# Softmax attention on one core: value products of two key tiles in one visit, four buffers of exponentials

## The chip, the cores and the metric

One core of one Trainium2 chip. The metric is the device time of one execution of the program, in microseconds (us). Less than about 0.5% of it can't be told from no change.

## The reference

A two-layer block over `x` (16 batches, 56 rows, 128 features) with a context of 1500 rows a batch: linear attention, a quantized feed-forward, softmax attention, a mixture of 8 experts. The change lies in the softmax attention of the second layer. It has 16 heads of 8 features:

```python
scores = jnp.einsum('bhqd,bhkd->bhqk', qh, kh) / jnp.sqrt(jnp.float32(D_K))
scores = jnp.where(m == 0, jnp.float32(NEG_INF), scores)
attn = jax.nn.softmax(scores, axis=-1)
context = jnp.einsum('bhqk,bhkd->bhqd', attn, vh)
```

followed by an output projection with W_o. Here q comes from the normalized `x`, k and v from the context, and the mask is over the 1500 keys.

## The kernel before

The program is one unrolled stream of instructions for each engine, with semaphores between them. It has three stages: the linear attention over the context of all batches and the feed-forward (up to about 328 us), the softmax attention (328 to about 766 us), and the experts. All of the change is in the second.

**Windows and tiles.** The softmax attention runs 16 windows, one for each batch, written as pairs (`pair1`): the first and the last pair are unrolled, those between are a loop on each engine. A window has T = 12 key tiles of TK = 125 keys. The scores are held transposed, keys on partitions: for one tile `scores` (line 578) does 8 matmuls of 112 columns (two heads' 56 queries), four in each of two halves, into PSUM banks 0, 1 (even tiles) or 2, 3 (odd tiles). ScalarE turns both banks into exponentials in one instruction (`exponentials`, line 818, the activation on line 825) and writes them to one of two buffers `P[t % 2]`, 125 x 896 in float32. `weigh` (line 594) multiplies the values of the tile, `Vp`, with them: 8 matmuls (16 instructions in the profile, as they are float32) of 32 stationary columns each, placed in four column groups of the array, which add into PSUM bank 7 over the 12 tiles. `Vp` has a column of ones, so that the sums of the exponentials come out with the products. This text calls one call of `weigh` a value product.

**Units.** Between the scores and the value products TensorE does other work of the neighbouring windows, one unit at a time, in a list written out by hand (`PLACES`, lines 55 to 57). In window w:

- MX0 to MX20: plain score products (line 492) for window w+1, 128 queries x 500 keys each, of which VectorE takes the maximum (line 1222). From the maxima comes the shift of the exponentials.
- SH: the row of shifts (line 502), which VectorE copies into the stack of queries QS of window w+1 (line 1228).
- DEN and WO: the division by the sums and the output projection of window w-1 (lines 507 and 513); VectorE takes DEN with a reciprocal (line 1231) and WO with a copy.
- K0 to K2: the key projection for window w+2 (line 478). ScalarE takes it (line 776), VectorE makes the remainder (`key_rest`, line 1099).
- V0 to V2: the value projection for window w+1 (line 484), which ScalarE copies into `Vp` (line 769).

MX, SH, DEN and WO share PSUM banks 4 and 5 by turns: each waits until VectorE has emptied the unit two before it. K and V share bank 6, one at a time. Each tile has three places for units:

```python
PLACES = [["MX0", "MX1", "V0"], ["MX2", "MX3", "MX4"], ["DEN", None, "V1"], ["MX5", "MX6", "V2"],
          ["MX7", "WO", "K0"], ["MX8", "MX9", "MX10"], ["MX11", "MX12", "K1"], ["MX13", "MX14", "MX15"],
          ["MX16", "MX17", "K2"], ["MX18", "MX19", "MX20"], [None, None, None], ["SH", None, None]]
```

**Order on TensorE** (`window`, line 606): for each tile t, the first half of its scores, the unit of place 0, the second half, the unit of place 1, the value product of tile t-1 (in tile 0: of tile 11 of the window before), the unit of place 2. TensorE takes its instructions in this order, and an unmet wait holds all that stands behind it.

**Waits.** Scores of tile t wait for the exponentials of tile t-2 (their banks), exponentials of tile t for the scores of t and the value product of t-2 (their buffer), the value product of t for the exponentials of t. The first scores of a window also wait for the row of shifts and for the transfers of the stacks. After the exponentials of tile 0, ScalarE takes the finished sums of the window before (`take_sums`, line 829); the value product of tile 0 waits for that, as it writes the same bank.

**Transfers.** The scores use keys and queries stacked in bfloat16 parts. GpSimd makes the last part of the keys of window w+1 (line 918) after ScalarE's part (line 781), which it casts at tile 10 of window w-1. Then SP issues six transfers that stack the keys (line 335, 375 KB each), six that stack the queries (line 339), and the load of the context for window w+2 (line 327).

The tiles `xn` and `t0` (128 x 8 x 128, float32) are used by the normalizations before and after the softmax attention, not in it.

Of the kernel before, what the change touches and what calls it, by code (L numbers as in the profile page):

```python
# [6 lines left out]
ACT = mybir.ActivationFunctionType  # L7
# [5 lines left out]
B, S, D = 16, 56, 128  # L13
S2 = 1500
H, DK = 16, 8
T, TK = 12, 125
# [8 lines left out]
HQ = H * S  # L25
# [4 lines left out]
PAIRW = 2 * S  # L30
PW = 32
NPAIR = H // 2
SLOTS = 2 * NG
KVW = D + H
EPS_LN, EPS_IN = 1e-5, 1e-6
ROUND = 12582912.0
# [31 lines left out]
def units(w, of=None):  # L68

    if not isinstance(w, int):  # L70
        now = ALL
    elif w < 0:
        now = EARLY + MXS + ["SH"]
    elif w >= B - 1:
        now = ENDS
    else:
        now = [u for u in ALL if not (w == 0 and u in ENDS) and not (w == B - 2 and u[0] == "K")]
    return [u for u in now if of is None or kind(u) == of]
# [40 lines left out]
def in_pairs(eng, body, pairs):  # L119

    body(0)
    with eng.Fori(1, pairs - 1) as i:
        body(i)
    body(pairs - 1)


def build(nc, xh, ctxT, m0, m1, gates, rows, bq, bk, wkv0, wq0, dense0, wg0, wu0, wd0, wq1, wk1, wv1, wo1,
          gatew, w1, b1, w2, b2, bv, ident_in, hmask_in, hmask1_in, pmask_in,
          den_sel_in, rank_in, out):
    with ExitStack() as ctx:  # L130
        def sb(name, shape, dt=F32):
            return ctx.enter_context(nc.sbuf_tensor(name, shape, dt))
# [3 lines left out]
        def sem(name):  # L136
            if name not in sems:
                sems[name] = ctx.enter_context(nc.semaphore(name))
            return sems[name]
# [3 lines left out]
        xn = sb("xn", [128, NT, D])  # L143
        t0 = sb("t0", [128, NT, D])
# [46 lines left out]
        cT = [sb(f"cT{n}", [128, S2]) for n in range(2)]  # L191
        kvall = sb("kvall", [128, B, KVW])
        kvtmp = sb("kvtmp", [128, 2, D])
# [39 lines left out]

        Qb = [sb(f"Qb{n}", [128, H, S], BF16) for n in range(2)]
        Vp = [sb(f"Vp{n}", [128, T, NPAIR, PW]) for n in range(2)]
        P = [sb(f"P{n}", [128, HQ]) for n in range(2)]
        mx = sb("mx", [128, CH, KC])
        mneg = sb("mneg", [128, CH], BF16)
        O = sb("O", [128, 2 * PAIRW])
# [149 lines left out]
        def _(pe):  # L389
# [23 lines left out]
            def y_group(b, par, g, first):  # L413
                n = NG * b + g
                if g == 0:
                    pe.wait_ge(sem(f"ctx0_in{par}"), loads(b, par))
                if first:
                    if g == 0:
                        pe.wait_ge(sem("wkv_ready"), 1)
                    if g == 2:  # L420
                        pe.wait_ge(sem("q0T_ready"), 2)
                else:
                    pe.wait_ge(sem("kn_ready"), n - 2)
                    pe.wait_ge(sem("vn_ready"), n - 2)
                for t in range(GT):
                    c0 = (GT * g + t) * TK
                    ins = nc.tensor.matmul(ps2[0:TK, 1024 * g + 256 * t:1024 * g + 256 * t + 256],  # L427
                                           cT[par][:, c0:c0 + TK], wkv[:].rearrange("p k d -> p (k d)"),
                                           start=True, stop=True)
                ins.then_inc(sem("y_ready"), 1)  # L430
# [13 lines left out]

            pe.sem_inc(sem("kv_done"), SLOTS)
            y_group(0, 0, 0, True)
# [72 lines left out]
            for b in range(B):  # L519
                t, r = b // 2, HALF * (b % 2)  # L520
                ins = nc.tensor.matmul(ps[r:r + HALF, t // 3, KVW * (t % 3):KVW * (t % 3) + KVW],
                                       qT[:, HALF * b:HALF * b + HALF], kvall[:, b, :], start=True, stop=True)
# [55 lines left out]
            def scores(b, par, t, k, first):  # L578

                n = b * T + t  # L580
                if t == 0 and k == 0:
                    pe.wait_ge(sem(f"stacked{par}"), loads(b, par, 2 * STACK))
                    pe.wait_ge(sem(free_of(b - 1, "SH")), emptied(b - 1, "SH"))
                if k == 0 and not (first and t < 2):
                    pe.wait_ge(sem("p_ready"), n - 1)
                for p in range(4 * k, 4 * k + 4):
                    c0 = S2 * p + TK * t
                    ins = nc.tensor.matmul(ps[:, 2 * (t % 2) + k, PAIRW * (p % 4):PAIRW * (p % 4) + PAIRW],  # L588
                                           KS[par][:, c0:c0 + 128], QS[par][:, PAIRW * p:PAIRW * p + PAIRW],
                                           start=True, stop=True)  # L590
                if k == 1:
                    ins.then_inc(sem("sc_ready"), 1)

            def weigh(b, par, t, first):
                n = b * T + t
                pe.wait_ge(sem("p_ready"), n + 1)
                if t == 0 and not (first and par == 0):
                    pe.wait_ge(sem("o_ready"), b)
                for p in range(NPAIR):
                    r, c = PW * (p % 4), PAIRW * (p // 4)  # L600
                    ins = nc.tensor.matmul(ps[r:r + PW, 7, c:c + PAIRW], Vp[par][0:TK, t, p, :],  # L601
                                           P[t % 2][0:TK, PAIRW * p:PAIRW * p + PAIRW],
                                           start=(t == 0 and p < 4), stop=(t == T - 1), skip_group_check=True)
                ins.then_inc(sem("pv_done"), 1)

            def window(w, par, first_pair):

                def unit_at(t, place):
                    unit = PLACES[t][place]
                    if unit in units(w):  # L610
                        b = w - 1 if unit in ENDS else w + 2 if unit[0] == "K" else w + 1
                        fill(w, unit, b, par if unit[0] == "K" else 1 - par)

                first = first_pair and par == 0
                for t in range(T):
                    scores(w, par, t, 0, first)
                    unit_at(t, 0)
                    scores(w, par, t, 1, first)
                    unit_at(t, 1)
                    if t > 0:  # L620
                        weigh(w, par, t - 1, first_pair)
                    elif not first:
                        weigh(w - 1, 1 - par, T - 1, first_pair)
                    unit_at(t, 2)

            pe.wait_ge(sem("filled"), 1)
# [6 lines left out]
                    window(2 * i + par, par, fixed and i == 0)  # L633

            in_pairs(pe, pair1, B // 2)
            weigh(B - 1, 1, T - 1, False)
            fill(B, "DEN", B - 1, 1)
            fill(B, "WO", B - 1, 1)

# [67 lines left out]
        def _(act):  # L707
# [26 lines left out]
            def deviation(n, k):  # L734
                act.wait_ge(sem("ss_ready"), n + 1)
                nc.scalar.activation(sdk[0:TK, k % 2, :], ss[0:TK, k % 2, :], ACT.Sqrt,
                                     bias=eps_in[0:TK, :]).then_inc(sem("sdk_ready"), 1)
# [10 lines left out]
            def pair(i):  # L748
                first = isinstance(i, int) and i == 0
                for par in range(2):  # L750
                    for g in range(NG):
# [3 lines left out]
                        if not (first and k < 1):  # L755
                            values(n - 1, (k - 1) % SLOTS)
                        deviation(n, k)

            in_pairs(act, pair, B // 2)
            values(NG * B - 1, SLOTS - 1)  # L760
            act.wait_ge(sem("setup_in"), 80)
# [56 lines left out]
            def exponentials(b, par, t, first):  # L818
                n = b * T + t
                act.wait_ge(sem("sc_ready"), n + 1)  # L820
                if not (first and t < 2):
                    act.wait_ge(sem("pv_done"), n - 1)
                act.wait_ge(sem("kb_ready"), 1)
                src = ps[0:TK, 2 * (t % 2):2 * (t % 2) + 2, 0:HQ2]
                nc.scalar.activation(P[t % 2][0:TK, :].rearrange("p (k n) -> p k n", k=2), src, ACT.Exp,  # L825
                                     scale=kscale[0:TK, bass.ds(n, 1)],
                                     bias=kbias[0:TK, bass.ds(n, 1)]).then_inc(sem("p_ready"), 1)

# [127 lines left out]
        def _(dve):  # L956
# [89 lines left out]
            def state(b, par):  # L1046

                dve.wait_ge(sem("kv_done"), NG * (b + 1) + SLOTS)
                kv = ps[:, 6 + par, :]
                v.tensor_tensor(kvtmp[:, par, :], kv[:, 0:D], gmask[:], ALU.mult).then_inc(sem("kvt_ready"), 1)  # L1050
                v.tensor_scalar(kvall[:, bass.ds(b, 1), D:KVW], hmask[:].unsqueeze(1), kv[:, D + 1:D + 2], None,
                                ALU.mult)
# [4 lines left out]
            def pair(i):  # L1057
                first = isinstance(i, int) and i == 0
                for par in range(2):
                    b = 2 * i + par  # L1060
                    for g in range(NG):
                        n, k = NG * b + g, NG * par + g
                        norms(n, k)
                        if not (first and k < 2):
                            relu(n - 2, (k - 2) % SLOTS)
                        if g == 0 and not first:
# [4 lines left out]
            last = NG * B - 1  # L1071
            relu(last - 1, SLOTS - 2)
            relu(last, SLOTS - 1)
# [6 lines left out]
            def nd(t):  # L1080
                return ps[:, t // 3, KVW * (t % 3):KVW * (t % 3) + KVW]

            for t in range(NT):
                ins = v.tensor_scalar(xn[:, t, 0:H], nd(t)[:, D:KVW], EPS_IN, None, ALU.add)
            step(ins)
# [338 lines left out]
```

## Time and profile before

| what | us |
|---|---|
| runs | 888.0, 891.3, 892.58 (median 891.3) |
| profiled execution: span (no other time of this execution is given) | 888.3 |
| TensorE busy | 715.8 |
| VectorE busy | 590.6 |
| ScalarE busy | 482.0 |
| GpSimd busy | 251.1 |
| the softmax attention, first scores to the last window's end | 328 to 766 |

The profile names engines PE (TensorE's matmuls), PEld (its weight loads, which overlap the matmuls), DVE (VectorE), ACT (ScalarE), POOL (GpSimd) and SPq (SP's queue of transfers). A row of a timeline has the start, the length, the engine, the line, the operation with output <- input, the shapes and a count of merged instructions. In brackets stands how long the engine was idle before it and what ended that. The length of a merged row reaches from the first start to the last end; ends of matmuls are modelled and overlap the next start, so that the text goes by starts.

### The profile page before, as it was taken

What the parts mean: (1) busy time and instruction counts of PE and PEld (TensorE: products, weight loads), DVE (VectorE), ACT (ScalarE), POOL (GpSimd) and SP (SyncE); (2) the same over time, 40 slices, a digit from 0 to 9 for tenths busy, and PEclk for the clock granted to TensorE, in tenths of its full rate; (3) what the DMA queues carried; (4) which work ended last, traced back from release to release, by engine and by line L of the source; (5) the groups of instructions that cost most, each with busy time, mean ns of one, the idle gap of its engine ahead of it and who ended that gap; (6) DMA issues with size and microseconds to landing.
All of it is one profiled execution on the core that took longest, in us unless ns stands there. A gap on an engine that the chain in (4) does not pass through costs nothing.

```text
span 888.3 us, 19613 instructions
## 1 busy us (share of the span) xinstructions
PE 715.8 (81%) x7277; PEld 492.1 (55%) x7277; DVE 590.6 (66%) x1145; ACT 482.0 (54%) x718; POOL 251.1 (28%) x236
## 2 busy tenths in 40 slices
PE   1588888876436478986799999999999997699998
PEld 1466666665222225653565566666566664457776
DVE  7699999996678676754567676668677675421111
ACT  1366666663225316664567766767666675463332
POOL 7177777774100540220122102222202210000000
PEclk9899999997565759997999999999999999889999
DMA  3122222141770074894959898899998977011101
GB/s 121 35 70 70 69 69 69 69 147 35 58 87 1 0 118 74 103 126 68 106 92 126 116 127 118 122 125 123 122 139 101 126 80 113 10 48 47 47 26 33
DMA packets 59459, 74.16 MB, mean 83 GB/s; under 512 B 35308, under 2 KB 40166, under 8 KB 59422
## 3 DMA queue, kind: packets, MB, share of 16 engines
q1 hardware_dynamic: 59422, 73.65, 52.9%
q8 instruction: 25, 0.41, 0.2%
q14 instruction: 12, 0.10, 0.0%
HBM read 32.61 MB, written 1.40 MB: 38 GB/s over the span
## 4 chain that ended last, share of the span: by engine, by line
PE 48%; DVE 30%; issue 11%; DMA 5%; SPq 3%; ACT 3%; DVEq 1%; POOL 0%; ACTq 0%
PE ps L601 7%; PE ps L492 7%; DVE ss L1023 6%; PE ps L588 6%; PE ps L659 6%; PE ps L671 6%; DVE mx L1222 6%; PE ps L484 5%; PE ps L478 5%; DMA QS<-QD 3%; DVE arena L1038 3%; DVE arena L1044 2%; DVE xn L977 2%; PE ps L513 2%; DVE wv L1034 1%
## 5 line engine op out<-in xcount | busy, mean ns | idle before, releaser
L1222 DVE TENSOR_REDUCE mx<-ps 128x1 f32<-128x500 f32 x336 | 215.0, 674 | 115.4 <-PE ps L492 113.9
L825 ACT ACTIVATE P<-ps,kbias,kscale 125x896 f32<-125x896 f32 x192 | 210.4, 1097 | 97.3 <-PE ps L588 93.0
L918 POOL TENSOR_TENSOR KP<-kvall,KP 128x1500 bf16<-128x1500 f32 x16 | 48.5, 3031 | 344.8 <-ACT KP L781 344.8
L492 PE MATMUL ps<-KP,Qb 128*128 128x500 bf16 x336 | 135.3, 404 | 9.7 <-issue 4.4
L601 PE MATMUL ps<-P,Vp 125*32 125x112 f32 x3072 | 116.4, 269 | 3.1 <-issue 1.7
L427 PE MATMUL ps<-wkv,cT 128*125 128x256 f32 x384 | 91.9, 383 | 0.8 <-ACT arena L744 0.8
L601 PEld LDWEIGHTS ps<-P,Vp 125*32 125x32 f32 x3072 | 68.6, 110 | 42.9 <-issue 36.0
L441 PE MATMUL ps<-arena 125*128 125x130 f32 x384 | 57.6, 294 | 37.3 <-DVE arena L1044 34.5
L744 ACT ACTIVATE arena<-ps,wv 125x128 f32<-125x128 f32 x192 | 54.8, 368 | 58.0 <-DVE arena L1038 58.0
L441 PEld LDWEIGHTS ps<-arena 125*128 125x128 f32 x384 | 48.2, 196 | 56.1 <-DVE arena L1044 52.8
L588 PE MATMUL ps<-QS,arena 128*128 128x112 bf16 x768 | 67.5, 215 | 12.5 <-issue 6.1
L588 PE MATMUL ps<-QS,KS 128*128 128x112 bf16 x768 | 70.4, 218 | 9.0 <-DVE QS L1228 4.6
L588 PEld LDWEIGHTS ps<-QS,KS 128*128 128x128 bf16 x768 | 55.4, 101 | 39.8 <-issue 24.3
L902 POOL TENSOR_TENSOR arena<-arena,row 125x512 f32<-125x512 f32 x48 | 61.1, 1272 | 54.0 <-DVE arena L1038 54.0
L588 PEld LDWEIGHTS ps<-QS,arena 128*128 128x128 bf16 x768 | 52.7, 99 | 41.5 <-issue 25.6
L427 PEld LDWEIGHTS ps<-wkv,cT 128*125 128x125 f32 x384 | 69.2, 190 | 10.0 <-issue 1.2
L776 ACT ACTIVATE KP<-ps,bk_sb 128x500 bf16<-128x500 f32 x48 | 32.5, 677 | 76.3 <-PE ps L478 76.3
L869 ACT ACTIVATE arena<-ps,b 128x448 f32<-128x448 f32 x64 | 40.4, 633 | 47.9 <-PE ps L659 42.1
L478 PE MATMUL ps<-cT,wk_sb 128*128 128x500 f32 x96 | 58.4, 693 | 9.8 <-issue 6.7
L905 POOL TENSOR_TENSOR arena<-arena,row 125x512 f32<-125x512 f32 x48 | 64.2, 1337 | 3.8
L1338 DVE SCALAR_TENSOR_TENSOR t<-ps,pgd,t 128x128 f32<-128x128 f32 x56 | 16.0, 345 | 70.1 <-PE ps L671 70.1
L1023 DVE TENSOR_REDUCE ss<-arena 125x8 f32<-125x1024 f32 x48 | 57.9, 1205 | 3.6 <-ACT arena L731 3.6
(189 smaller groups left out, 1038.8 us busy)
## 6 DMA issues: line engine op xcount, KB each, us to landing
cT<-ctxT_dram SPq DMA_DIRECT2D x32, 750.0 KB, 4.4
KS<-KP SPq DMA_DIRECT2D x48, 375.0 KB, 12.9
arena<-KP SPq DMA_DIRECT2D x48, 375.0 KB, 12.9
QS<-QD SPq DMA_DIRECT2D x96, 28.0 KB, 15.9
wgu<-w_dram SPq DMA_DIRECT2D x8, 256.0 KB, 2.8
silu<-w_dram SPq DMA_DIRECT2D x8, 256.0 KB, 2.6
x<-xh_dram SPq DMA_DIRECT2D x1, 512.0 KB, 3.3
mixed<-att SPq DMA_DIRECT2D x16, 28.0 KB
```

What stands on the lines that cost most here:

```text
L427: ins = nc.tensor.matmul(ps2[0:TK, 1024 * g + 256 * t:1024 * g + 256 * t + 256], cT[par][:, c0:c0 + TK], wkv[:].rearrange("p k d -> p (k d)"),
L441: ins = nc.tensor.matmul(ps[:, 6 + par, 0:D + 2], KN[0:TK, s6, t, :], VN[0:TK, s6, t, :], start=(g == 0 and t == 0), stop=(g == NG - 1 and ...
L478: ins = nc.tensor.matmul(ps[:, bank, 0:KCW], wk1_sb[:], cT[par][:, KCW * k:KCW * k + KCW], start=True, stop=True)
L492: ins = nc.tensor.matmul(ps[:, bank, 0:KCW], q[:, 128 * c:128 * c + 128], KP[par][0][:, KCW * k:KCW * k + KCW], start=True, stop=True)
L588: ins = nc.tensor.matmul(ps[:, 2 * (t % 2) + k, PAIRW * (p % 4):PAIRW * (p % 4) + PAIRW], KS[par][:, c0:c0 + 128], QS[par][:, PAIRW * p:PA ...
L601: ins = nc.tensor.matmul(ps[r:r + PW, 7, c:c + PAIRW], Vp[par][0:TK, t, p, :], P[t % 2][0:TK, PAIRW * p:PAIRW * p + PAIRW], start=(t == 0 ...
L744: ins = nc.scalar.activation(VN[0:TK, k, t, 0:D], ps2[0:TK, c0:c0 + D], ACT.Copy, scale=wv[0:TK, k % 2, t:t + 1])
L825: nc.scalar.activation(P[t % 2][0:TK, :].rearrange("p (k n) -> p k n", k=2), src, ACT.Exp, scale=kscale[0:TK, bass.ds(n, 1)], bias=kbias[0 ...
L902: nc.gpsimd.tensor_tensor(kn, kn, bc(row[0:TK, GAMMA, :], 1, [TK, GT, D]), ALU.mult).then_inc(sem("kg_ready"), 1)
L905: nc.gpsimd.tensor_tensor(kn, kn, bc(row[0:TK, BETA, :], 1, [TK, GT, D]), ALU.add).then_inc(sem("kb0_ready"), 1)
L1023: v.tensor_reduce(ss[0:TK, k % 2, :], SQ[0:TK, k % 2, :].rearrange("p (j d) -> p j d", d=D), AX.X, ALU.add).then_inc(sem("ss_ready"), 1)
L1222: ins = v.tensor_reduce(mx[:, c, k:k + 1], ps[:, bank, 0:KCW], AX.X, ALU.max)
```

## The change

Every second tile does two value products, one after the other. In even tiles t that is those of t-2 and t-1 (in tile 0: of tiles 10 and 11 of the window before); odd tiles do none. After the last window the last two are done together. The exponentials get four buffers in place of two, `P[t % 4]`; the two new ones lie over `xn` and `t0`. The exponentials of tile t wait for the value product of t-4.

```diff
+PB = 4
...
-        P = [sb(f"P{n}", [128, HQ]) for n in range(2)]
+        P = [sb(f"P{n}", [128, HQ])[:] for n in range(2)]
+        P += [a[:].rearrange("p t d -> p (t d)")[:, 0:HQ] for a in (xn, t0)]
...
-                                           P[t % 2][0:TK, PAIRW * p:PAIRW * p + PAIRW],
+                                           P[t % PB][0:TK, PAIRW * p:PAIRW * p + PAIRW],
...
-                    if t > 0:
-                        weigh(w, par, t - 1, first_pair)
-                    elif not first:
-                        weigh(w - 1, 1 - par, T - 1, first_pair)
+                    if t % 2 == 0:
+                        for back in (2, 1):
+                            if t > 0:
+                                weigh(w, par, t - back, first_pair)
+                            elif not first:
+                                weigh(w - 1, 1 - par, T - back, first_pair)
                     unit_at(t, 2)
...
-            weigh(B - 1, 1, T - 1, False)
+            for back in (2, 1):
+                weigh(B - 1, 1, T - back, False)
...
-                if not (first and t < 2):
-                    act.wait_ge(sem("pv_done"), n - 1)
+                if not (first and t < PB):
+                    act.wait_ge(sem("pv_done"), n - PB + 1)
...
-                nc.scalar.activation(P[t % 2][0:TK, :].rearrange("p (k n) -> p k n", k=2), src, ACT.Exp,
+                nc.scalar.activation(P[t % PB][0:TK, :].rearrange("p (k n) -> p k n", k=2), src, ACT.Exp,
```

## Rows read from the trace of the kernel before

**Rows 1.** The page: TensorE's busy time, and the chain that ended last by engine.

```profile
PE 715.8 (81%) x7277; PEld 492.1 (55%) x7277; DVE 590.6 (66%) x1145; ACT 482.0 (54%) x718; POOL 251.1 (28%) x236
...
PE 48%; DVE 30%; issue 11%; DMA 5%; SPq 3%; ACT 3%; DVEq 1%; POOL 0%; ACTq 0%
```

**Rows 2.** By window: length; busy PE, PEld, DVE, ACT, POOL; clock; DMA share, GB/s.

```profile
453.84:480.64 26.80, 25.11 (x357) 16.36 (x358) 19.07 (x31) 19.07 (x21) 6.21 (x6) 1.00 0.91 116
...
586.77:613.03 26.26, 25.10 (x357) 16.36 (x358) 19.05 (x31) 18.00 (x21) 5.13 (x6) 1.00 0.94 125
613.03:639.84 26.81, 25.11 (x357) 16.37 (x358) 19.07 (x31) 19.08 (x21) 6.22 (x6) 1.00 0.92 120
...
692.88:720.68 27.80, 26.66 (x357) 17.50 (x358) 19.15 (x31) 18.11 (x21) 5.12 (x6) 0.94 0.81 94
```

**Rows 3.** Timeline, tiles 1 to 4 of the window at 586.77: start, length, engine.

```profile
589.49 0.37 PE L492 MATMUL ps<-KP,Qb 128*128 128x500 bf16 x1
...
591.22 0.65 PE L507 MATMUL ps<-O,den_sel 128*128 128x224 f32 x2
...
592.51 1.14 PE L484 MATMUL ps<-wv_sb,cT 128*125 128x128 f32 x8
...
593.69 0.62 ACT L769 COPY Vp<-ps 125x512 f32<-125x512 f32 x1 [0.39 <-PE ps L484]
...
594.92 1.14 PE L484 MATMUL ps<-wv_sb,cT 128*125 128x128 f32 x8
...
595.89 0.36 PE L588 MATMUL ps<-QS,arena 128*128 128x112 bf16 x4
...
596.09 0.37 PE L492 MATMUL ps<-KP,Qb 128*128 128x500 bf16 x1
...
596.30 0.36 PE L588 MATMUL ps<-QS,arena 128*128 128x112 bf16 x4
```

**Rows 4.** Timeline, tiles 5 to 7 of the same window.

```profile
599.26 0.37 PE L492 MATMUL ps<-KP,Qb 128*128 128x500 bf16 x1
...
601.65 0.10 PEld L492 LDWEIGHTS ps<-KP,Qb 128*128 128x128 bf16 x1 [0.24 <-DVE mx L1222]
...
601.97 0.35 PEld L601 LDWEIGHTS ps<-P,Vp 125*32 125x32 f32 x16 [0.22 <-issue]
...
602.49 0.30 PEld L478 LDWEIGHTS ps<-cT,wk_sb 128*128 128x128 f32 x2 [0.17 <-issue]
...
603.63 0.37 PE L492 MATMUL ps<-KP,Qb 128*128 128x500 bf16 x1
...
604.04 1.92 DVE L1222 TENSOR_REDUCE mx<-ps 128x1 f32<-128x500 f32 x3 [0.63 <-PE ps L492]
```

**Rows 5.** Timeline, tiles 9 to 11 of the same window and the next start.

```profile
608.00 0.37 PE L492 MATMUL ps<-KP,Qb 128*128 128x500 bf16 x1
...
611.21 0.37 PE L502 MATMUL ps<-identb,mneg 128*1 128x128 bf16 x8 [0.37 <-DVE mneg L1246]
...
611.63 1.27 DVE L1228 CAST QS<-ps 1x448 bf16<-1x448 f32 x2 [0.57 <-PE ps L502]
...
613.03 0.27 PE L588 MATMUL ps<-QS,KS 128*128 128x112 bf16 x2 [0.63 <-DVE QS L1228]
```

**Rows 6.** Timeline of TensorE cut inside one value product, and the whole product.

```profile
573.18 0.40 PE L601 MATMUL ps<-P,Vp 125*32 125x112 f32 x8
...
573.18 0.59 PE L601 MATMUL ps<-P,Vp 125*32 125x112 f32 x16
```

**Rows 7.** Line 339, 590 to 613.5: six query stacks, issue and time to landing.

```profile
L339 SPq DMA_DIRECT2D QS<-QD x6: 598/604/612, 594.4 to 597.6; - x6
...
DMA to landing us min/median/max: 15.2/16.2/17.3
```

**Rows 8.** Timeline of ScalarE in the last window.

```profile
759.34 2.12 ACT L825 ACTIVATE P<-ps,kbias,kscale 125x896 f32<-125x896 f32 x2 [0.16 <-PE ps L588]
```

**Rows 9.** Timeline of TensorE, a long gap in window 2.

```profile
407.68 2.04 PE L478 MATMUL ps<-cT,wk_sb 128*128 128x500 f32 x2 [6.70 <-issue]
```

## The prediction, made before the changed kernel ran

> **What bounds the kernel now.** I read the page first. [rows 1] TensorE is busy 81% of the span and the chain that ended last is 48% TensorE, 30% VectorE and 11% "issue": two engines hand work to each other, and no busy share alone says what an edit is worth. All of the change lies in the second attention, so the next view was the busy time by window (one batch of 12 key tiles, 16 in all, counted from 0) [rows 2]. Nine of them, from 453.84 to 692.88, take 239.04 us, 26.56 each, alternately 26.26 and 26.80, at full granted clock. The 16th has no maxima to make for a successor and is shorter.
>
> Then the timeline inside one window of 26.26 us. Five things are to be seen there.
>
> *Tiles 0 to 4* [rows 3]: TensorE goes from one operation to the next. The exception is tile 1: its three score products for the maxima (MX2, MX3, MX4) feed two PSUM banks that VectorE empties in 0.64 us each (three in 1.92, [rows 4]), and DEN at 591.22, which takes MX3's bank, starts 1.73 us after MX2 at 589.49, just when VectorE has got through MX2 and MX3 (0.41 until it starts, 2 × 0.64, 0.04 or so for the signal).
>
> *Tiles 5 to 8* [rows 4]: from MX8 at 599.26 to MX12 at 601.65 are 2.39 us, and MX12 waited for VectorE: 0.41 + three reductions in 1.92 + 0.06. From MX12 it is TensorE's turn: 0.32 to the value product, 0.52 for it, 1.14 for the key projection and four score products, and MX13 starts at 603.63, 1.98 us after MX12. VectorE idles 0.63 meanwhile. The pair of tiles 7 and 8 repeats it, in 4.37 us each.
>
> *Tiles 9 to 11* [rows 5]: from MX18 at 608.00 to the next window at 613.03 are 5.03 us, all of it behind VectorE: three reductions, the rest of the key parts, the largest of the maxima, and then, after TensorE's turn at 611.21, the row of shifts (two copies, 1.27 us, from 611.63), for which the next window's first scores wait. Three value products lie in that time and cost nothing.
>
> *One value product* [rows 6]: 16 instructions in 0.59 us, the first 8 in 0.40. So each 8 take 0.19 at the steady pace, though a product set between other operations displaces 0.52 behind it and 0.1 ahead of it: weight loads stand idle 0.22 before its own and 0.17 before the next operation's [rows 4].
>
> *The transfers* [rows 7]: the stacks of the queries for the window at 613.03 were issued from 594.4 to 597.6 and landed 15.2 to 17.3 us later, so by about 612.8. That is just in time. The issue starts after GpSimd's key remainder, which hangs on the end of the window before. This makes a second loop over two windows, of 26.26 + 26.80 = 53.06 us [rows 2], against 52.5 for the compute loop; it is what makes every other window 0.54 longer.
>
> **The change part by part.** No product is removed: a window has 6 double visits instead of 12 single ones. Odd tiles lose theirs; even tiles do that of t-2 and of t-1 (tile 0: tiles 10 and 11 of the window before).
>
> *A double visit* costs 16 more matmuls in an even tile. Bounds: 0.35 (the 16 weight loads of a block) and 0.52 (a whole lone block), both [rows 4]. I take 2 × 0.19 = 0.38, the steady pace, because nothing but already met waits stands between the two tiles.
>
> *Tile 0*: +0.38, on TensorE's path.
>
> *Tile 1*: the product goes, but MX4 needs MX2's bank and DEN needs MX3's: MX2 to DEN stays 1.73. 0.00. TensorE stands still where it worked.
>
> *Tile 2*: +0.38. DEN, scores and V1 are all TensorE's.
>
> *Tile 3* is the one real gain. V1 to V2 is 2.40 now (592.51 to 594.92). Without the product TensorE needs 0.98 for V1, four scores 0.20, MX5 0.21, four scores 0.20, MX6 0.21: 1.80 (0.98, 0.20 and 0.21 by 594.92, 595.89, 596.09 and 596.30). But V2 takes the one side bank that ScalarE empties: its copy starts 1.18 after V1 (593.69) and takes 0.62, with the signal 1.85. So the gain is 2.40 - 1.85 = 0.55.
>
> *Tile 4*: +0.38. The values' last part of ScalarE stays ahead of the next user.
>
> *Tiles 5 and 7*: the product lies between MX9 and MX10 (MX14 and MX15), inside the 2.39 us that VectorE sets: 0.00 for each. *Tiles 6 and 8*: the double visit lies after MX12 (MX17), where VectorE waits for TensorE: +0.38 each.
>
> *Tiles 9, 10, 11*: under VectorE's 5.03 us. The cover: tile 10's double visit would end near 610.8, the shifts come at 611.21. 0.00; without that cover it would cost another 0.4.
>
> Sum: 5 × 0.38 - 0.55 = **+1.35 us a window**: 27.61 for the compute loop.
>
> *The transfer loop*: only the stretch up to the window's end grows, by 1.35, so two windows need 53.06 + 1.35 = 54.41 by transfers and 55.22 by compute. It stops binding, and its 0.54 in every other window is swallowed.
>
> *Four buffers*: two are laid over tiles that are idle in this stage; no instruction is added. The exponentials wait for the product four tiles back instead of two. ScalarE isn't late: in tiles 5 to 8 it idles too, and tile t's scores wait for exponentials t-2 as before. The doubled visit ends each pair's use of exponentials later, which two more buffers cover; without them ScalarE would wait in each odd tile.
>
> *ScalarE and the queues*: ScalarE takes the finished sums after tile 0's visit, which ends 0.38 later; what it does next, the copy of V0, is 0.38 later by TensorE anyway. No DMA is moved and SP and GpSimd are passed by nothing.
>
> *Last window*: here ScalarE sets the pace: two exponentials in 2.12, then 0.16 idle, 2.28 a pair [rows 8]. With the change one exponential of each pair still comes after a product and eight scores: 0.00, at most 0.1 a pair.
>
> Total: nine windows 9 × 27.61 - 239.04 = +9.5. Windows 1 to 3, 13 and 14, whose starts show no transfer wait: 5 × 1.35 = +6.8. Window 0 has no visit in tile 0 and no DEN: +0.9. Sum **+17.2**. The profile has gaps "issue" of several us in some windows (one of 6.70, [rows 9]) which the change doesn't address. The profiled execution's span is 888.3; no other time of that execution is shown, and the span lies within the runs' 888.0 to 892.6, so I put the sum on the median: 891.3 + 17.2 = **908.5**.
>
> **A rule against the forecast.** The trace shows 0.22 and 0.17 us of idle weight loading around a product [rows 4]. The Trainium skill, TensorEngine Tiling (Array Packing), Key Properties, says that a change of tiling mode, though not of tile, drains the engine; these products use 32 of 128 columns and their neighbours 128. By that rule alone, with every saved drain on the path, the sum would be rival A's; the trace agrees that a switch costs something, 0.24 a pair by the terms above, but not that it is waited for.
>
> **The rivals.** *A, the saved switches reach the end (faster).* Place: each odd tile. Price: a visit costs 0.1 + 0.52, its second half in a double one 0.38, so 0.24 is saved six times a window, 1.4. That would need VectorE and ScalarE to be early enough at MX4, MX10, MX12, MX15, MX17 and V2; it decides if the 2.39 us shrink. By TensorE alone: 14 × 1.4 = 20 less. But of the 1.4, 1.2 lies ahead of the key part that releases the transfers, and that loop then needs (53.06 - 1.2)/2 = 25.9 a window, 0.6 less, in nine of them; with 5 × 1.4 in the others about 12 in all, **879**. For it: the idle loads. Against it: MX12's wait for VectorE in all windows. Chance 0.10. The Trainium skill's rule above, taken alone, gives the same.
>
> *B, the two cancel (no change).* Place: tiles 5 to 8. If the second half of the double visit is hidden there, under a VectorE that is late at MX13 too, the two +0.38 go and tile 3's gain stays: 3 × 0.38 - 0.55 = 0.6 a window, half of which the transfer wait swallows in nine of them: +6, **897**; with a gain of tile 1's half us it is 892. Against it: VectorE idles 0.63 ahead of MX13 [rows 4], more than the 0.38. Chance 0.13, 0.08 of it within 0.5%.
>
> *C, the clock falls as well.* TensorE works 1.4 us less and waits 2.8 more in each longer window. Window 13 had a granted clock of 0.94 and took 27.80 where its like takes 26.26 [rows 2]: 1.5 each. In six or more windows it makes **918** and up. Chance 0.07.
>
> *D, the second product isn't at the steady pace* (0.52, as alone): 75 visits × 0.14 = +10: **919**. Part of the forecast's upper end.
>
> **How the numbers follow.** Forecast 0.70, A 0.10, B 0.13, C 0.07. A measurement of this kernel can tell about 0.5% (4.5 us) from nothing. Slower by more: 0.70 + 0.07 + 0.05 of B = 0.82; within: 0.08; faster: 0.10. The lower bound of the visit (0.35) gives 906, gaps of "issue" move by some us in either direction; the range 896 to 917 takes in the upper half of B and part of C and D.
>
> **What would show it.** Right: windows of 27.6 without alternation; MX8 to MX12 still 2.39; MX12 to MX13 2.36 in place of 1.98; value products as 32 in about 0.97; V1 to V2 1.85; "DVE mx" as releaser of TensorE in tiles 1, 5, 7 for about 0.5 more; busy TensorE down by some 10 us at most. Wrong: MX8 to MX12 shorter, or windows under 26.3 (A); windows of 26.5 to 27 (B); granted clock under 0.95 in many windows (C); 32 matmuls in over 1.05 (D).

## The result and the profile after

| | before | after |
|---|---|---|
| runs, us | 888.0 to 892.58, median 891.44 (4) | 899.27 to 901.86, median 900.48 (4) |
| profiled execution: its time, its span | as in the table of before, 888.3 | 901.86, 900.1 |

The ratio is 1.011, with a 95% interval of 1.008 to 1.0139: the change makes the kernel slower by 9 us. The forecast was 908.5, in a range of 896 to 917. Between the two profiled executions the difference is 11.8 us of span; the profiled one of after was the slowest of its four.

TensorE does the same products in 5 us less busy time, and the span is 11.8 longer (the row of the page that answers to the first of [rows 1]):

```profile
PE 710.8 (79%) x7276; PEld 499.7 (56%) x7277; DVE 586.2 (65%) x1145; ACT 482.1 (54%) x718; POOL 251.2 (28%) x236
```

By window (the columns of [rows 2]):

```profile
457.24:484.70 27.46, 24.83 (x358) 16.82 (x358) 18.85 (x31) 18.54 (x21) 5.68 (x6) 1.00 0.90 118
...
594.42:621.82 27.40, 24.77 (x357) 16.82 (x358) 18.84 (x31) 18.55 (x21) 5.69 (x6) 1.00 0.90 118
621.82:649.22 27.40, 24.77 (x358) 16.83 (x358) 18.86 (x31) 18.55 (x21) 5.69 (x6) 1.00 0.90 118
...
731.42:762.30 30.88, 23.79 (x352) 16.47 (x352) 17.09 (x28) 15.89 (x17) 2.68 (x1) 0.89 0.85 116
```

The two things forecast of the windows are there. They are longer, 27.4 where the windows of before took 26.26 and 26.80 by turns, and the alternation is gone. The nine windows from the one that starts at 457.24 take 246.82 us (to 704.06) against 239.04: +7.8. Window 14, the last row, took 30.88 at a clock of 0.89, with a gap "issue" of 4.86 in it; its counterpart took 27.91 at 0.94, with a gap of 3.69.

The timeline of tiles 1 to 4 of the window at 594.42, which answers to [rows 3]:

```profile
597.52 0.37 PE L494 MATMUL ps<-KP,Qb 128*128 128x500 bf16 x1
...
598.67 0.38 PE L494 MATMUL ps<-KP,Qb 128*128 128x500 bf16 x1 [0.37 <-DVE mx L1227]
...
599.25 0.30 PEld L509 LDWEIGHTS ps<-O,den_sel 128*128 128x128 f32 x2 [0.16 <-DVE mx L1227]
599.25 0.65 PE L509 MATMUL ps<-O,den_sel 128*128 128x224 f32 x2
...
600.02 0.97 PE L603 MATMUL ps<-P,Vp 125*32 125x112 f32 x32
...
600.93 1.14 PE L486 MATMUL ps<-wv_sb,cT 128*125 128x128 f32 x8
...
602.78 0.95 PEld L486 LDWEIGHTS ps<-wv_sb,cT 128*125 128x125 f32 x8 [0.22 <-ACT Vp L774]
```

In tile 1 TensorE now stands still for VectorE 0.37 us ahead of MX4, and ahead of DEN its weight load waits for VectorE again (0.16); MX2 to DEN is 1.73 as before. The double visit is one block of 0.97, which holds up V1 by 0.91 (600.02 to 600.93). V1 to V2 is 1.85, with 0.22 of it a wait for ScalarE's copy of V1.

Tiles 5 to 7, which answer to [rows 4]:

```profile
607.50 0.37 PE L494 MATMUL ps<-KP,Qb 128*128 128x500 bf16 x1
...
607.92 1.85 DVE L1227 TENSOR_REDUCE mx<-ps 128x1 f32<-128x500 f32 x3 [1.88 <-PE ps L494]
...
608.65 0.39 PE L494 MATMUL ps<-KP,Qb 128*128 128x500 bf16 x1 [0.37 <-DVE mx L1227]
...
609.82 0.10 PEld L494 LDWEIGHTS ps<-KP,Qb 128*128 128x128 bf16 x1 [0.16 <-DVE mx L1227]
...
610.14 0.73 PEld L603 LDWEIGHTS ps<-P,Vp 125*32 125x32 f32 x32 [0.22 <-issue]
...
611.04 1.10 PE L480 MATMUL ps<-cT,wk_sb 128*128 128x500 f32 x2
...
612.18 0.37 PE L494 MATMUL ps<-KP,Qb 128*128 128x500 bf16 x1
```

MX12 to MX13 went from 1.98 to 2.36 us: the second product's 0.38. MX8 to MX12, which I had taken as fixed at 2.39, is 2.32. Three reductions take 1.85 in place of 1.92.

Tiles 9 to 11 and the next start, which answer to [rows 5]:

```profile
616.86 0.37 PE L494 MATMUL ps<-KP,Qb 128*128 128x500 bf16 x1
...
618.71 0.97 PE L603 MATMUL ps<-P,Vp 125*32 125x112 f32 x32
...
620.42 1.27 DVE L1233 CAST QS<-ps 1x448 bf16<-1x448 f32 x2 [0.57 <-PE ps L504]
...
621.82 0.37 PE L590 MATMUL ps<-QS,KS 128*128 128x112 bf16 x4 [1.15 <-DVE QS L1233]
```

MX18 to the next start is 4.96 (5.03 before). The double visit of tile 10, at 618.71, lies in its cover. The stacks of queries for the window at 621.82 landed by 605.8 + 15.2 = 621.0, 0.8 before it started ([rows 7]):

```profile
L341 SPq DMA_DIRECT2D QS<-QD x6: 598/599/604, 602.5 to 605.8; - x6
...
DMA to landing us min/median/max: 15.2/16.2/17.2
```

### The profile page after: what moved, and what is told of

Same layout as the page of the kernel before. It is cut to its first block, busy times and chain, and to the rows that moved or that the text cites. A ratio compares the mean times of both kernels' runs of the same rounds, so it can differ in the third digit from the quotient of the medians.

```text
span 900.1 us, 19642 instructions
## 1 busy us (share of the span) xinstructions
PE 710.8 (79%) x7276; PEld 499.7 (56%) x7277; DVE 586.2 (65%) x1145; ACT 482.1 (54%) x718; POOL 251.2 (28%) x236
## 4 chain that ended last, share of the span: by engine, by line
issue 43%; DVE 24%; PE 20%; POOL 5%; DMA 3%; SPq 2%; ACT 1%; DVEq 1%; POOLq 0%; ACTq 0%
DVE ss L1028 6%; PE ps L676 6%; PE ps L664 6%; DVE arena L1043 3%; POOL Qb L931 2%; DVE arena L1049 2%; DVE xn L982 2%; DMA QS<-QD 2%; POOL QD L935 1%; PE ps L494 1%; DVE wv L1039 1%; PE ps L603 1%; PE ps L395 1%; SPq L317 1%; DVE mx L1227 1%
## 5 line engine op out<-in xcount | busy, mean ns | idle before, releaser
L1227 DVE TENSOR_REDUCE mx<-ps 128x1 f32<-128x500 f32 x336 | 210.2, 672 | 131.7 <-PE ps L494 130.3
L494 PE MATMUL ps<-KP,Qb 128*128 128x500 bf16 x336 | 134.8, 403 | 28.5 <-DVE mx L1227 23.9
L830 ACT ACTIVATE P<-ps,kbias,kscale 125x896 f32<-125x896 f32 x96 | 105.4, 1097 | 55.8 <-PE ps L590 54.0
L443 PE MATMUL ps<-arena 125*128 125x130 f32 x384 | 58.5, 297 | 36.2 <-DVE arena L1049 33.4
L494 PEld LDWEIGHTS ps<-KP,Qb 128*128 128x128 bf16 x336 | 33.2, 99 | 69.2 <-DVE mx L1227 62.2
L830 ACT ACTIVATE xn<-ps,kbias,kscale 125x896 f32<-125x896 f32 x48 | 52.7, 1098 | 26.7 <-PE ps L590 26.7
```

What stands on the lines that cost most here:

```text
L443: ins = nc.tensor.matmul(ps[:, 6 + par, 0:D + 2], KN[0:TK, s6, t, :], VN[0:TK, s6, t, :], start=(g == 0 and t == 0), stop=(g == NG - 1 and ...
L494: ins = nc.tensor.matmul(ps[:, bank, 0:KCW], q[:, 128 * c:128 * c + 128], KP[par][0][:, KCW * k:KCW * k + KCW], start=True, stop=True)
L830: nc.scalar.activation(P[t % PB][0:TK, :].rearrange("p (k n) -> p k n", k=2), src, ACT.Exp, scale=kscale[0:TK, bass.ds(n, 1)], bias=kbias[ ...
L1227: ins = v.tensor_reduce(mx[:, c, k:k + 1], ps[:, bank, 0:KCW], AX.X, ALU.max)
```

## Experiments

The theory: a value product costs what its place makes it cost; in even tiles the double visit stands where TensorE is waited for, in odd tiles the room it leaves is filled by waits. Each run was made beside runs of the kernel before on the same chip, and ratios are to those. The times of whole executions move by several us with gaps "issue" and with the granted clock, so what is said of the mechanism rests on the lengths of single windows at full clock, which agree to 0.1 us inside an execution (transfer waits apart). "The nine steady windows" are windows 4 to 12, 239.04 us in the profile of the kernel before; what a kernel gains outside them can come from the gaps and the clock alone.

**Four buffers alone.** The value product is back in each tile:

```diff
-                    if t % 2 == 0:
-                        for back in (2, 1):
-                            if t > 0:
-                                weigh(w, par, t - back, first_pair)
...
+                    if t > 0:
+                        weigh(w, par, t - 1, first_pair)
```

> One value product in each tile as in the kernel before, but four buffers of exponentials, two of them over xn and t0, and exponentials that wait for the product four tiles back. Theory (place): the loss comes from where the double visits stand, the buffers cost nothing: windows of 26.26 and 26.80 by turns, 891 us, within 0.5% of the kernel before. Rival (buffers or ScalarE's waits): a part of the +9 us is here already, windows over 26.8 without alternation, 895 or more.

Measured: 888.86 us, ratio 0.9966 (0.9933 to 0.9999). The buffers cost nothing. Windows alternate as in the kernel before; some, like the third row, took 1.55 more at a clock of 0.94:

```profile
502.61:529.39 26.78, 25.10 (x358) 16.37 (x358) 19.06 (x31) 19.04 (x21) 6.18 (x6) 1.00 0.93 121
529.39:555.64 26.25, 25.09 (x357) 16.35 (x358) 19.05 (x31) 18.03 (x21) 5.15 (x6) 1.00 0.94 125
582.43:610.24 27.81, 26.65 (x357) 17.50 (x358) 19.14 (x31) 18.13 (x21) 5.14 (x6) 0.94 0.90 121
```

**Double visits one tile later.**

```diff
-                    if t % 2 == 0:
-                        for back in (2, 1):
-                            if t > 0:
-                                weigh(w, par, t - back, first_pair)
...
+                    if t == 0 and not first:
+                        for back in (2, 1):
+                            weigh(w - 1, 1 - par, T - back, first_pair)
+                    elif t % 2 == 1 and t > 1:
+                        for back in (3, 2):
+                            weigh(w, par, t - back, first_pair)
```

> The changed kernel with five of the six double visits one tile later: products of t-3 and t-2 in the odd tiles 3 to 11, that of the last two tiles in tile 0 as before. Same number of visits, same instructions. Theory (place): they now lie where TensorE waits for VectorE. Per window against the kernel before: tile 0 +0.38, tile 2 -0.62, tile 3 +0.38, tile 4 -0.62, tiles 5 and 6 -0.26, tiles 7 and 8 -0.26, MX20 late by 0.37, sum -0.6: compute loop 25.65, transfer loop (53.06 - 0.6)/2 = 26.2, so windows of 26.2 and about 885 us. Rival (a double visit costs its own time wherever it is put): windows of 27.4 and 900 us again.

Measured: 889.05 us, ratio 0.9967 (0.9939 to 0.9996). With as many double visits as the changed kernel, its execution has none of the loss; a double visit doesn't cost the same wherever it is put. But the windows are 26.7, not 26.2, so that 0.45 of the changed kernel's 1.14 over the compute loop of 26.26 is still there, and the nine steady windows take 240.8, no less than before:

```profile
586.61:613.32 26.71, 24.24 (x357) 16.58 (x358) 19.03 (x31) 18.26 (x21) 5.61 (x6) 1.00 0.93 123
613.32:640.10 26.78, 24.24 (x357) 16.59 (x358) 19.05 (x31) 18.39 (x21) 5.75 (x6) 1.00 0.92 120
```

The size was off for a wait that I had overlooked. In its timeline (tiles 7 and 8) the key projection at 606.76 waited for VectorE's remainder of the keys (line 1104), which empties bank 6 and comes only after three reductions, which the double visit had delayed. MX13 to MX18 (603.34 to 607.90) is 4.56, where I had worked out 4.11:

```profile
604.05 0.97 PE L603 MATMUL ps<-P,Vp 125*32 125x112 f32 x32
...
604.96 0.39 PE L494 MATMUL ps<-KP,Qb 128*128 128x500 bf16 x1
...
606.76 1.10 PE L480 MATMUL ps<-cT,wk_sb 128*128 128x500 f32 x2 [0.26 <-DVE kvall L1104]
...
607.90 0.37 PE L494 MATMUL ps<-KP,Qb 128*128 128x500 bf16 x1
```

**Products left out, in odd or in even tiles.**

```diff
                 pe.wait_ge(sem("p_ready"), n + 1)
+                if t in (2, 4, 6, 8, 10):
+                    pe.wait_ge(sem("pv_done"), n)
+                    pe.sem_inc(sem("pv_done"), 1)
+                    return
```

and the same with `(1, 3, 5, 7, 9)`.

> The kernel before without the products of key tiles 2, 4, 6, 8 and 10, which it does in tiles 3, 5, 7, 9 and 11; nothing stands in their place but the signal. Theory (place): they cost 0.55 in tile 3, 0.07 each in tiles 5, 7 and 9 and nothing in tile 11, 0.77 a window; nine windows go by transfers at (53.06 - 0.77)/2 = 26.15: about 883 us. Rival (TensorE is the bound, each product costs its 0.62): 3.1 a window, transfers at 25.2, about 865 us.

> The kernel before without the products of key tiles 1, 3, 5, 7 and 9, which it does in tiles 2, 4, 6, 8 and 10. Theory (place): 0.62 each in tiles 2, 4, 6 and 8, nothing in tile 10: 2.5 a window, transfers at (53.06 - 2.5)/2 = 25.3 in nine windows: about 869 us, nearly three times the gain of leaving out the same number in odd tiles. Rival (each product costs alike): the same time as without those in odd tiles.

Measured: 874.15 us (ratio 0.9796, 0.974 to 0.9853) without those in odd tiles, 870.29 (0.9759, 0.9705 to 0.9813) without those in even tiles. The totals don't decide between the theories: the first saved twice what I expected and the second about what I expected. The windows tell why. Without the products of odd tiles, and then window 2 of the kernel before:

```profile
379.69:408.10 28.41, 25.65 (x278) 16.33 (x278) 19.00 (x31) 17.67 (x20) 3.31 (x5) 0.89 0.88 117
...
517.09:543.85 26.76, 22.83 (x278) 14.61 (x278) 18.83 (x31) 19.07 (x21) 6.96 (x6) 0.98 0.91 118
543.85:571.98 28.13, 25.49 (x278) 16.36 (x278) 18.98 (x31) 18.12 (x20) 4.38 (x6) 0.89 0.89 119
```

```profile
384.47:420.69 36.22, 28.44 (x358) 18.05 (x358) 19.27 (x31) 18.17 (x21) 2.43 (x5) 0.83 0.69 92
```

Window 2 took 28.4 where the kernel before took 36.2. The gaps "issue" of over 1.2 us, five in the profile of the kernel before with 19.3 us together, are not in this one; why they went wasn't found out. The steady windows, meanwhile, are longer than before, up to 28.13: every second one waits over 2.4 us for transfers at its end, and in the next the granted clock is 0.89 to 0.94. The nine take 245.9 us without the products of odd tiles and 241.4 without those of even tiles, against 239.04: in neither kernel does any of the saving lie in them. What the products themselves cost is read inside a window. Without that of tile 3, V1 to V2 is 1.85 (-0.55, as expected). Without that of tile 5, tiles 5 and 6 take 4.29 in place of 4.37 (-0.08, as expected). In the kernel without the products of even tiles, tile 2 takes 1.89 in place of 2.54 (0.09 of which comes back in tile 3), tile 4 2.65 in place of 3.17, and tile 6 2.52 in place of 2.71: -0.19 and not the -0.62 expected. There the key projection waits for the remainder again:

```profile
564.13 1.10 PE L478 MATMUL ps<-cT,wk_sb 128*128 128x500 f32 x2 [0.26 <-DVE kvall L1103]
```

So in tiles 6 and 8 adding a product costs 0.38 but taking one away gives back 0.19: another wait stands right behind TensorE's work. What a product costs does hang on its tile: 0.56, 0.08 and 0.08 for those done in tiles 3, 5 and 7, and 0.57, 0.52, 0.19 and 0.19 for those in tiles 2, 4, 6 and 8.

**Earlier key stacks.** To read the compute loop by itself, the transfers were moved out of its way, in the kernel before and in the changed one:

```diff
-                sp.wait_ge(sem("kp3_ready"), b + 1)
                 for j, part in enumerate(KEY_PART):
+                    if j in (0, 5):
+                        sp.wait_ge(sem("kp2_ready" if j == 0 else "kp3_ready"), b + 1)
                     sp.dma_start(
```

> The kernel before, with the first five of the six transfers that stack the keys issued when ScalarE's part of them is there, and only the sixth waiting for GpSimd's remainder: the stacking starts about 2.8 us earlier in each window. Theory (the alternation of 26.26 and 26.80 is a wait for transfers, and 26.26 is the compute loop): all windows of 26.26, the stacks landed 2 us or more before a window starts, 2.4 us less in nine windows, about 0.3%. Rival (the alternation has another cause, or the transfers are bound by what they move and not by when they start): windows alternate as before and the time is the same.

> The changed kernel with the same earlier issue of the key stacks. Theory: its windows of 27.4 are set by TensorE and VectorE, the transfers have slack already, so nothing changes: windows of 27.40, within 0.3% of the changed kernel's 900.5. Rival (part of the loss is a wait for transfers): windows under 27.4.

Measured: 886.48 us, ratio 0.9926 (0.9903 to 0.9948), for the kernel before with it; 899.3, ratio 1.0081 to the kernel before (1.005 to 1.0112), for the changed one, whose own time was 900.48. Windows of the first, and its query stacks, landed by 611.3, 2.8 ahead of the start at 614.11:

```profile
561.58:587.85 26.27, 25.11 (x358) 16.38 (x358) 19.06 (x31) 18.54 (x21) 5.68 (x6) 1.00 0.94 124
587.85:614.11 26.26, 25.09 (x358) 16.36 (x358) 19.05 (x31) 18.53 (x21) 5.67 (x6) 1.00 0.94 124
```

```profile
L340 SPq DMA_DIRECT2D QS<-QD x6: 598/606/617, 592.9 to 596.1; - x6
...
DMA to landing us min/median/max: 15.2/16.2/17.3
```

A window of the second:

```profile
621.33:648.77 27.44, 24.81 (x357) 16.82 (x358) 18.84 (x31) 18.52 (x21) 5.67 (x6) 1.00 0.90 118
```

The compute loops are 26.26 and 27.44. The 0.54 in every other window of the kernel before was a wait for transfers, and the change hides it behind its own +1.18; the changed kernel gains nothing from earlier stacks. The nine steady windows of the kernel before gained 2.7 by them, where 2.4 was expected; its time fell by 0.7% where 0.3% was expected, and the rest of that isn't explained.

**Halves of the change.** With earlier stacks, double visits in tiles 0, 2 and 4 only; in tiles 6, 8 and 10 only; and in tile 4 only. A table says which tiles each visit takes:

```diff
+VISITS = [(2, 1), (), (2, 1), (), (2, 1), (1,), (1,), (1,), (1,), (1,), (1,), ()]
...
+                    for back in VISITS[t]:
+                        if t > 0:
+                            weigh(w, par, t - back, first_pair)
+                        elif not first:
+                            weigh(w - 1, 1 - par, T - back, first_pair)
```

> Kernel before with earlier key stacks (its windows then are 26.26), and the change in tiles 11 and 0 to 4 only: double visits in tiles 0, 2 and 4 (and for the last two tiles after the last window), single ones in tiles 5 to 10. Theory: tile 0 +0.38, tiles 1 and 2 +0.38, tile 3 -0.55, tile 4 +0.38: windows of 26.85. Rival (the double visits of tiles 6 and 8 carry the loss, the head breaks even): 26.3.

> Kernel before with earlier key stacks, and the change in tiles 5 to 10 only: double visits in tiles 6, 8 and 10, none in 5, 7 and 9, single ones elsewhere. Theory: +0.31 for each of the pairs 5, 6 and 7, 8 (0.385 for the second product, 0.075 back since MX10 and MX15 come in time), -0.075 for MX20: windows of 26.80, and with the other half the whole 1.14. Rival (the loss is all in the head): 26.3.

> Kernel before with earlier key stacks, and a single double visit: none in tile 3, the products of tiles 2 and 3 in tile 4. Theory (a double visit gains where TensorE is the one waited for at both places): +0.385 - 0.556 = -0.17 a window: 26.09. Rival (a double visit always loses): 26.3 or more.

Measured: the first 905.17 us, ratio 1.0153 (1.0043 to 1.0263), from two runs. Its second row is one of four windows of 28.3 to 28.5 at a clock of 0.94:

```profile
571.13:597.99 26.86, 24.81 (x357) 16.53 (x358) 19.08 (x31) 18.54 (x21) 5.67 (x6) 1.00 0.92 121
597.99:626.41 28.42, 26.37 (x357) 17.54 (x358) 19.16 (x31) 18.65 (x21) 5.66 (x6) 0.94 0.87 114
```

The second 889.97, ratio 0.998 (0.9946 to 1.0013), and the third 889.47, ratio 0.995 (0.9929 to 0.9971):

```profile
587.16:613.97 26.81, 25.05 (x357) 16.66 (x358) 18.83 (x31) 18.54 (x21) 5.67 (x6) 1.00 0.92 121
```

```profile
609.80:635.89 26.09, 24.93 (x357) 16.40 (x358) 19.06 (x31) 18.53 (x21) 5.67 (x6) 1.00 0.95 124
```

At full clock the windows are 26.86, 26.81 and 26.09: +0.60, +0.55 and -0.17 on 26.26, where 26.85, 26.80 and 26.09 had been worked out. The two halves add up to 1.15, all of the change's 1.14 to 1.18. One double visit in tile 4, with tile 3 left empty, shortens the window: there both products had been on TensorE's path, so that the saved switch counts. This holds of the windows and not of the totals. The half in tiles 0 to 4 came out no faster than the whole change (1.0153, on two runs, against 1.0081), with its windows at 0.94 and a gap "issue" of 6.26 in window 14, and the kernel with one double visit is no faster than the one with earlier stacks alone (0.995 against 0.9926), with a gap of 6.44 there.

**Products where TensorE waits.** The same table with other entries, without and with earlier stacks:

```diff
+VISITS = [(1,), (1,), (), (2,), (), (3,), (3,), (3,), (3,), (3,), (3, 2), (2, 1)]
```

> The kernel before with four buffers and the value products put where TensorE waits anyway: tiles 0, 1, 3, 5, 6, 7, 8 and 9 do one, tiles 2 and 4 none, tiles 10 and 11 two each. Same products. Theory (place): tile 2 gives about 0.57, tile 4 0.52, the rest stays, so the compute loop is 25.2; the transfer loop (53.06 - 1.1)/2 = 26.0 holds it back: about 881 us, with TensorE idle for over 2 us at window ends, after which the granted clock may fall for some us, as it did when products were left out: 881 to 888. Rival (the number of visits counts, not their place; here 12 products in 10 visits): at most 2 × 0.24 a window, about 886 with no dependence on place.

> The placement of the value products by waits, with the key stacks issued earlier as well. Theory: now neither the products nor the transfers hold the window back: windows of 25.2 to 25.4, 15 × 1.1 + 2.4 = 19 us less than before, about 872 us, granted clock 1.00 in the steady windows. Rival (the transfers are bound by what they move, 24.7 us of busy time a window): windows of 26 or more, 880 us or more.

Measured: 875.52 us, ratio 0.9805 (0.9768 to 0.9842), without earlier stacks, and **862.74, ratio 0.9671 (0.9642 to 0.97)**, with them. This version beats both kernels. Three windows without earlier stacks, then one with them:

```profile
577.09:602.27 25.18, 24.77 (x357) 16.43 (x358) 19.04 (x31) 17.77 (x20) 4.12 (x6) 1.00 0.98 130
602.27:629.06 26.79, 24.78 (x358) 16.43 (x358) 19.06 (x31) 18.85 (x21) 7.28 (x6) 1.00 0.92 120
629.06:655.74 26.68, 26.27 (x357) 17.64 (x358) 19.08 (x31) 17.76 (x20) 4.05 (x6) 0.94 0.94 126
```

```profile
567.55:592.72 25.17, 24.77 (x357) 16.43 (x358) 19.05 (x31) 18.30 (x21) 5.66 (x6) 1.00 0.98 129
```

The compute loop is 25.18, 1.08 less than 26.26 (1.1 expected). Without earlier stacks most windows wait for transfers up to 26.8, or run part of the time at the lower clock (third row): the nine steady ones take 239.09, as long as before, so that all of this version's gain (17 us, where 3 to 10 were expected) lies outside them. With earlier stacks the nine take 226.6, 12.4 less: 9 × 1.08 from the placement and 2.7 from the stacks. That the whole time fell by 30 us where 19 were expected comes from elsewhere: between the profiles windows 1 to 3 are 11.2 shorter where 3.3 was expected, with gaps "issue" of 9.7 in them in place of 14.4, and window 13 is 2.7 shorter where 1.1 was expected, as its counterpart ran at 0.94. With earlier stacks the DMA share is 0.98, so not much more is to be had that way.

## Why the prediction was right, and where its sizes were off

The direction, the mechanism and most terms held. Per window, at full clock:

| step of the prediction | forecast | measured |
|---|---|---|
| second product of a double visit | 0.38 | 0.38 (block of 0.97, MX12 to MX13 +0.38) |
| tile 0 | +0.38 | +0.38 |
| tiles 1 and 2 | 0.00 and +0.38 | -0.09 and +0.47, together +0.38 |
| tile 3 | -0.55 | -0.56 |
| tile 4 | +0.38 | +0.38 |
| tiles 5 and 6, 7 and 8 | +0.38 each pair | +0.31 each pair |
| tiles 9 to 11 | 0.00 | -0.08 |
| sum | +1.35 | +1.13 (windows: 27.40 - 26.26 = +1.14) |

(Measured in the windows at 586.77 and at 594.42: lengths of tiles, each from its first score product to that of the next.)

**The step that was mis-sized** is "Tiles 5 and 7 ... inside the 2.39 us that VectorE sets: 0.00". I read three reductions in 1.92 as VectorE at its own pace. It was not quite, and the 0.64 that I took for each is that mean: one takes 0.68, and two without a wait 1.25, so that one follows the other after 0.58 or so, as these rows of the kernel before show:

```profile
596.50 0.68 DVE L1222 TENSOR_REDUCE mx<-ps 128x1 f32<-128x500 f32 x1 [1.02 <-PE ps L492]
...
602.16 1.25 DVE L1222 TENSOR_REDUCE mx<-ps 128x1 f32<-128x500 f32 x2
```

The third waited some 0.07 for MX10, which the product had held back. Without the product the three take 1.85 (the timeline of tiles 5 to 7 above). The sign named for it, "MX8 to MX12 still 2.39", failed by as much, and the waits for "DVE mx" in tiles 1, 5 and 7 are 0.37 each instead of about 0.5. The product in an odd tile did cost 0.07, in three places a window: 0.22 of the 1.35, and some 3 us of the sum. What wait ends last had been read rightly for MX12, but the row of three merged reductions hid a wait inside it.

**The transfer loop** held: bound before, slack after, 0.54 swallowed in every other window (+7.8 in nine windows, where +9.5 was forecast; the difference is the term above, which alone would make 2.0).

**The other windows.** Windows 1 to 3, 13 and 14 took 6.2 more between the profiles (forecast 6.8), but partly by accident: windows 1 to 3 took 3.7 more, 3.0 is window 14 with its longer gap "issue" and lower clock, and window 13 took 0.4 less, since its counterpart had run at a clock of 0.94. Window 0, forecast +0.9, took 0.6 less: the kernel before had a gap "issue" of 1.24 in it. What follows the last window's start took 1.9 less, forecast 0; 0.7 of that is the last window up to its DEN. With 0.3 more ahead of window 0 these make 11.8 between the profiles; the medians differ by 9.0. Times move by that much from one execution to another: the 23 runs of the kernel before beside the first four experiments spread from 885.9 to 897.0, the shortest at a mean granted clock of 0.918, the longest at 0.906. Whether the gaps move too from run to run isn't on record, as each kernel has one profile.

**Rival A** (saved switches reach the end) had the prices of a single visit and of a second product right where TensorE is the one waited for: DEN to V1 is 0.61 shorter without the product done in tile 2, and a second product adds 0.38, which leaves about its 0.24. The one pair that was tried with both products on the path saved 0.17, as in tile 3 the product's going gives only 0.55 until V2 meets ScalarE's copy. For the change as made A's condition fails: MX8 to MX12 shrank by 0.07 and not by 0.24. The Trainium skill's rule of the drained array (TensorEngine Tiling (Array Packing), Key Properties) agrees with that saving in sign; that it is a drain which is saved no run shows. The rule says nothing on whether somebody waits for it, and that decided. **Rival B** is refuted by the halves: tiles 6 and 8 carry 0.55 of the 1.15. **Rival C** didn't happen in the changed kernel, whose windows 4 to 13 ran at 1.00 in its profile. **Rival D** is refuted by the 0.97.

The forecast of the time was high by 8 (17.2 against 9.0). Of this 5.4 lies between the profiles (17.2 against 11.8): 1.7 in the nine windows and 0.6 in the five others (the mis-sized term alone would make 3.1; 0.8 went the other way, in windows of 27.44 in place of 27.40, in the gaps and in the clock); 1.5 in window 0; 1.9 behind the last window's start; less the 0.3 ahead of window 0. The other 2.8 is the difference between the profiled executions and the medians, and what made it wasn't settled. With the term at its right size the sum would have been 905.4; the 5 us from there to the 900.5 measured no run explains, and the windows, 27.4 for 27.6, are the firmer test.

## What to carry to other kernels

Ask of each slot of an in-order engine who waits for what comes next there. Work taken out of a slot where the engine waits anyway gains little or nothing (here 0 to 0.08 of 0.62), and the same work put into a slot where others wait for it costs its full length, so that halving the switches can lose time. The same products, moved the other way and with the transfers issued earlier, made the steady windows 5% shorter than before (25.18 against 26.56 on average); of the 3.3% by which the whole time fell, less than two thirds is what the placement and the transfers had been expected to give (19 of 30 us). When a compute loop gets shorter, look for the next loop (here the transfers' issue) and free it in the same step, since windows that ended with TensorE idle for over 2.4 us were followed by windows at a lower granted clock (0.88 to 0.94). And look at where in the execution a gain lies before it is put down to the edit: three of the kernels here gained about 2% or more without a gain in the nine steady windows.

## What the runs showed that I had not expected

- Leaving work out made steady windows longer. Without the five products in odd tiles, every second window ended with TensorE idle for over 2.4 us, and the next ran at a granted clock of 0.89 to 0.94 and took up to 28.13 where compute alone would need less than 26.26. The version without earlier stacks, with 1.8 us idle, shows it in some windows (26.68 at 0.94, where 25.18 is its loop) and not in others (25.18 at 1.00, in the first of its rows).
- The clock also fell in single windows of kernels whose idle time at a window's end was only that of the kernel before: 27.81 at 0.94 against 26.25 at 1.00 inside one execution. Among windows 4 to 13 the number of such windows differed between kernels (one in the profile of the kernel before, none in the changed one, three and four in others). Why those windows wasn't found out.
- Gaps "issue" of 1.2 to 7.1 us differ between the profiles of the kernels (window 2: 36.2 in the kernel before, 28.4 with five products fewer), which moves the time of the execution by more than the change does in a window. In all of the profiles they lie in windows 0 to 3 and 14 alone: in the unrolled pairs and in the first pass of the loop, thus where TensorE comes to a stretch of its instructions for the first time, and in no later pass of the loop. No run tests what makes them.
